# A conditioned mixture-of-experts layer on one core: a new order of ScalarE's work while the expert weights are split, and a rotated loop over the routed tiles

## The reference

```python
c  = einsum('btd,od->bto', x, W) + (einsum(x, A[idx]) @ Bm[idx]) * scalings[idx]   # c: 4096 x 512
sh = einsum('ted,edh->th', gelu(einsum('th,ehd->ted', c, Wsh_up)), Wsh_down)       # 2 shared experts
probs = softmax(c @ W_router); top_v, top_i = top_k(probs, 2)
gate = sum(one_hot(top_i, 16) * top_v[..., None], axis=1)
rt = einsum('ted,edh->th', gelu(einsum('th,ehd->ted', c, Wrt_up)) * gate[:, :, None], Wrt_down)
out = x + sh + rt
```

## Time and profile before

| | |
|---|---|
| time, median of 3 runs | 681.92 us (681.80 to 685.59) |
| the profiled execution's own time | 681.92 us |
| span of its trace | 679.9 us |
| PE busy | 627.5 us, 92% |
| DVE busy | 457.4 us, 67% |
| ACT busy | 327.2 us, 48% |
| POOL busy | 222.6 us, 33% |
| mean granted TensorE clock | 0.974 |

### The profile page before, as it was taken

One profiled execution on the slowest core, in us unless ns is written; L12 is line 12 of the kernel. 1 busy time (PEld: TensorE's weight loads), 2 busy tenths in 40 slices (PEclk: granted clock), 3 DMA queues, 4 the chain that ended last, 5 costly groups with the idle time before them and its releaser, 6 DMA issues.

```text
span 679.9 us, 13742 instructions
## 1 busy us (share of the span) xinstructions
PE 627.5 (92%) x4115; PEld 428.4 (63%) x4117; DVE 457.4 (67%) x900; ACT 327.2 (48%) x480; POOL 222.6 (33%) x288
## 2 busy tenths in 40 slices
PE   4998999999989758889999999999999999989794
PEld 2465656566657435556777777777777777665561
DVE  2779999999974998525555555555555554688674
ACT  1333224677775743464555555555555554333230
POOL 1000000101012742373333333333333306777771
PEclk9997999999998988999999999999999999999898
DMA  7688994343334312165555555555555539989966
GB/s 275 281 312 286 374 346 168 123 157 142 132 127 128 124 63 93 32 217 171 159 159 169 161 154 159 164 168 157 156 159 167 164 107 377 366 301 362 369 205 248
DMA packets 49765, 135.68 MB, mean 200 GB/s; under 512 B 6160, under 2 KB 6288, under 8 KB 47312
## 3 DMA queue, kind: packets, MB, share of 16 engines
q1 hardware_dynamic: 38304, 97.93, 39.1%
q0 software_dynamic: 11440, 37.50, 20.0%
HBM read 86.38 MB, written 49.02 MB: 199 GB/s over the span
## 4 chain that ended last, share of the span: by engine, by line
PE 53%; DVE 17%; POOL 12%; issue 7%; DMA 7%; ACT 1%; SPq 0%; DVEq 0%; POOLq 0%; ACTq 0%
PE bank L1412 15%; PE bank L1393 14%; POOL rtw L608 9%; PE bank L1249 7%; PE bank L1377 5%; DVE lot_max L906 5%; DMA act_in<-xT 3%; PE bank L1402 2%; PE bank L1327 2%; PE bank L1257 2%; PE bank L1274 2%; DMA region<-xc_dram,slot_idx 2%; PE bank L1238 1%; DVE x_max L947 1%; PE bank L1265 1%
## 5 line engine op out<-in xcount | busy, mean ns | idle before, releaser
L1129 DVE SCALAR_TENSOR_TENSOR region<-bank,scale,region 128x512 f16<-128x512 f32 x79 | 59.2, 751 | 128.7 <-ACT region L809 128.7
L1393 PE MATMUL bank<-rtw,region 128*128 x948 | 116.4, 273 | 0.0
L1412 PE MATMUL bank<-rtw,tmp 128*128 x474 | 115.2, 379 | 0.6 <-DVE tmp L1137 0.6
L1393 PEld LDWEIGHTS bank<-rtw,region 128*128 128x128 f16 x948 | 92.8, 98 | 10.1
L1340 PE MATMUL bank<-shw,hid 128*128 128x512 f16 x384 | 91.3, 397 | 8.3 <-DVE rtw L1193 7.7
L574 POOL DMA_INDIRECT region<-xc_dram,slot_idx x79 | 77.1, 976 | 61.3 <-POOL slot_idx L571 61.3
L1327 PE MATMUL bank<-act_in,shw 128*128 128x256 f16 x768 | 89.4, 277 | 2.9 <-ACT tmp L756 1.7
L1327 PEld LDWEIGHTS bank<-act_in,shw 128*128 128x128 f16 x768 | 75.8, 100 | 16.0 <-ACT tmp L756 2.2
L816 ACT ACTIVATE region<-bank,un_dn 128x512 f32<-128x512 f32 x79 | 54.3, 687 | 57.3 <-PE bank L1412 54.8
L608 POOL DMA_INDIRECT rtw<-r_dram,row_idx x64 | 70.0, 1093 | 27.6 <-issue 14.8
L1340 PEld LDWEIGHTS bank<-shw,hid 128*128 128x128 f16 x384 | 38.4, 102 | 56.4 <-issue 10.0
(11 more groups left out here) (157 smaller groups left out, 910.0 us busy)
## 6 DMA issues: line engine op xcount, KB each, us to landing
r_dram<-region SPq DMA_DIRECT2D x79, 256.0 KB
rtw<-rt_w SPq DMA_DIRECT2D x16, 1024.0 KB, 7.4
act_in<-xT SPq DMA_DIRECT2D x16, 512.0 KB, 3.8
xc_dram<-rows SPq DMA_DIRECT2D x16, 512.0 KB, 3.7
xcT_dram<-hid SPq DMA_DIRECT2D x16, 512.0 KB, 2.8
rtw<-x_rows SPq DMA_DIRECT2D x16, 512.0 KB, 5.4
rtw<-xcT_dram SPq DMA_DIRECT2D x13, 512.0 KB, 6.1
out<-rtw SPq DMA_DIRECT2D x9, 512.0 KB, 5.6
```

Of the source, the lines that this page charges most:

```text
L1129: nc.vector.scalar_tensor_tensor(xgT[s][:, 1], R_XT[s][:].rearrange("p (k t) -> p k t", k=HK), col(scale, C_ALL).bitcast(F32), xgT[s][:, 0 ...
L1393: last = mm(R_UP[s][:, 0:D], xgT[s][:, xp, k, :], rtw[:, bass.ds(e, 1), w0:w0 + D].rearrange("p a d -> p (a d)"), start=(k == 0 and n == 0 ...
L1412: last = mm(R_DN[s][:], midT[s][:, xp, m, :], rtw[:, bass.ds(e, 1), w0:w0 + H].rearrange("p a h -> p (a h)"), start=(m == 0 and n == 0), s ...
```

## The change

It has two parts. In ACT's program, for chunks 8 to 15, the first of the two `high_routed` of a step moves ahead of `high_x`, the second directly behind it, and `cond_T` comes after both, directly ahead of `cond_rows`. In step 8, `high_x(9)` stays first, then one `high_routed`, `cond_T(7)`, the other, `cond_rows(8)`. In step 15, `high_condT(0)` comes ahead of `cond_T(14)`. In PE's program the round over two routed tiles begins with `r_transpose_mid` instead of `r_down`, and three registers are loaded instead of four; the loop has 36 rounds instead of 35.

```diff
-            def routed_step(i, s, more=True):
-                c = 2 * i + s
-                if more:
-                    high_x(c + 1, 1 - s)
-                cond_T(c - 1, i - 1 + s, 1 - s)
-                for e in range(2):
-                    high_routed(2 * c - NC + e)
-                if not more:
-                    high_condT(0, 0, C_EARLY, early=True)
-                cond_rows(i, s)
-
             high_x(NC // 2 + 1, 1)
+            act.wait_ge(scale_ready, 3)
+            high_routed(0)
             cond_T(NC // 2 - 1, A_HALF // 2 - 1, 1)
-            act.wait_ge(scale_ready, 3)
-            for e in range(2):
-                high_routed(e)
+            high_routed(1)
             cond_rows(A_HALF // 2, 0)
+
+            def routed_step(i, s):
+                high_routed(4 * i - NC + 2 * s)
+                high_x(2 * i + s + 1, 1 - s)
+                high_routed(4 * i - NC + 2 * s + 1)
+                cond_step(i, s)
+
             routed_step(A_HALF // 2, 1)
...
             for s in range(2):
-                routed_step(A_HALF - 1, s, more=s == 0)
+                high_routed(E_RT - 4 + 2 * s)
+                if s == 0:
+                    high_x(NC - 1, 1)
+                high_routed(E_RT - 3 + 2 * s)
+                if s:
+                    high_condT(0, 0, C_EARLY, early=True)
+                cond_step(A_HALF - 1, s)
...
-                    tile_e[0:1, bass.ds(i, 1), 0:4]...
+                    tile_e[0:1, bass.ds(i, 1), 0:3]...
...
-            def r_round(i, first=False):
+            def r_pair(i, first=False, more=True):
                 e = r_experts(i)
                 for s in range(2):
                     j = 2 * i + s
-                    r_down(j, s, e[s], first)
-                    r_transpose_mid(j + 1, 1 - s, first and s == 0)
-                    r_up(j + 2, s, e[2 + s])
-                    r_transpose_x(j + 4, i + 2, s)
+                    r_transpose_mid(j, s, first and i == 0)
+                    r_up(j + 1, 1 - s, e[s + 1], first and i == 0 and s == 0)
+                    if more:
+                        r_transpose_x(j + 3, i + 1 + s, 1 - s)
+                    if first and i == 0 and s == 0:
+                        pe.wait_ge(shared_ready, NT * EARLY)
+                    r_down(j, s, e[s], first and i == 0)
...
-            e = r_experts(0)
-            r_up(0, 0, e[0], first=True)
+            r_up(0, 0, r_experts(0)[0], first=True)
             r_transpose_x(2, 1, 0)
-            r_transpose_mid(0, 0, first=True)
-            r_up(1, 1, e[1], first=True)
-            r_transpose_x(3, 1, 1)
-            pe.wait_ge(shared_ready, NT * EARLY)
             for i in range(2):
-                r_round(i, first=(i == 0))
-            with pe.Fori(2, NJ_2 - 2) as i:
-                r_round(i)
...
+                r_pair(i, first=True)
+            with pe.Fori(2, NJ_2 - 1) as i:
+                r_pair(i)
+            r_pair(NJ_2 - 1, more=False)
+
+            e = r_experts(NJ_2)
             r_transpose_mid(NJ - 1, 0)
             shared_up(EARLY // 2, 0, blocks=range(1))
-            r_down(NJ - 1, 0, e[2])
+            r_down(NJ - 1, 0, e[0])
```

More of the change, by code:

```diff
@@ L1382, in r_experts @@
                 return nc.values_load_multi_w_load_instructions(
-                    tile_e[0:1, bass.ds(i, 1), 0:4].rearrange("p a m -> p (a m)"), engines=(mybir.EngineType.PE,), min_val=0, max_val=E_RT - 1,
+                    tile_e[0:1, bass.ds(i, 1), 0:3].rearrange("p a m -> p (a m)"), engines=(mybir.EngineType.PE,), min_val=0, max_val=E_RT - 1,
                     skip_runtime_bounds_check_because="a count of experts, cut off at the last one by the vector engine")[1]
```

## The result

The changed kernel takes 745.75 us (median of 4 runs, 742.05 to 749.36), the one before 683.75 us in the same session: a ratio of 1.0906, 95% interval 1.0838 to 1.0976. The forecast was 726 with a range of 708 to 740. The direction and the mechanism of ScalarE's part came out, the size did not: some 20 us come from TensorE's part, which I had priced at nothing.

A forecast was written before the change was run, and what follows sets the result against it. In chunks 8 to 15 PE was taken as the bound, DVE nearly full; routed tiles were a gapless PE rhythm. 681.9 + 26.8 (loop) + 17.6 (clock) + 0 (tile order) = 726.3, forecast 726 us, range 708 to 740.

The forecast's parts named there:

- The closed loop: Chunks 8 to 15: PE, DVE and ACT wait in a ring, 14.9 us a step against 10.86; +26.8 us at full clock.
- The view of the waits: Steps 8 to 15: ACT waits for DVE directly ahead of `cond_T`, no longer for PE's transposes; DVE waits for `high_x`.
- the reversal of who waits for whom: Steps 8 to 15: PE's router waits for DVE, DVE for ACT, and ACT for PE through `cond_rows`; no separate size.
- the stage view: Steps 8 to 15 were to show 15 to 19 us each, PE idle 3 to 5 us ahead of the first router matmul.
- one sign: Steps 8 to 15: DVE was to be seen waiting for ACT's `high_x`; no size given.
- Part 1: ACT's new order in steps 8 to 15: +26.8 us from the loop and +17.6 us from the clock.
- Rival (c): Steps 8 to 15: the stall is paid only at the start, +7 us, 689 us; chance 0.07.
- (d): Steps 8 to 15: early `high_routed` fills ACT's idle time and PE's 1.29 and 2.08 us bubbles vanish, 678.5 us; chance 0.03.
- The clock: Steps 8 to 15: PE's clock falls after each of 8 stalls, 2.2 us each, +17.6 us; bounds 0 and 26.9.
- Rival (a): Steps 8 to 15: the loop closes but PE keeps its clock or pays a small ramp, 709 to 716 us; chance 0.14.
- Part 2: Routed tiles: PE's reordered loop end stays hidden, 0 us over 36 rounds; bounds a gain of 0 and a loss of 7.2.
- Rival (b): Routed tiles: the loop-end work is not hidden, 733 us, or 745 at full exposure; chance 0.12.

The follow-up runs named there:

- e7: e1 plus 14 extra unused matmuls on PE ahead of each router product in steps 8 to 15; 712.4 us, ratio 1.0472 to the kernel before.
- e5: e1 with `high_x` moved ahead of the first `high_routed` from step 9 on; 721.9 us, ratio 1.0592 to the kernel before.
- e10: e5 plus 10 extra matmuls in PE's idle time ahead of the router; 701.3 us, ratio 1.0304 to the kernel before.
- e1: The kernel before with only ScalarE's (ACT's) new order, TensorE's loop unchanged; 731.3 us, ratio 1.0674.
- e9: ScalarE's part alone, `cond_T` between the two `high_routed` from step 9 on, step 8 in its old order; 681.1 us, ratio 0.9967.

## Why the prediction was wrong, point by point

**The closed loop: right, in place and in size.** At full clock the step was to be 14.9 us; the steps of the changed kernel less their clock share are 14.92 and 14.95, e7 has one of 15.0. The view of the waits, the reversal of who waits for whom, and the stage view came as described, but for one sign: DVE waited for `high_x` in four steps only, 3.1 us in all. Part 1 alone is +46 us where the sum of its terms was 44.4; so close a total is luck in part, since the loop's term was too large and the clock's too small, as the next point shows. Rival (c), a stall only at the start, and (d), the other side, fall by the same rows: each of the 8 routers waits.

**The clock: right in kind, sized too small.** The term was 8 x 2.2 = 17.6 us. From router to adapter inputs the 8 pairs took 6.54, 6.76, 6.98, 6.44, 6.82, 6.99, 5.06 and 6.33 us, less 3.50 each: together 23.9 us, 3.0 a stall. I had thought that part of each low stretch would fall in slack; mostly it did not, and the value lay near the bound of 3.36. In return the rest of the stage came to 47.9 - 23.9 = 24.0 us, not 26.8; 1.1 of that is step 8, where the scales came earlier against PE's work (router +2.4 us, not +3.5), and 1.5 is step 9, which took 14.8 us less its clock share, not 16.3: the rows of chunk 8 waited for PE's slow adapter products, so some of the low stretch did fall in slack there. Rival (a) falls. The Trainium skill's rule ("TensorE: Matmul & The Clock Gate", section "What's actually happening"), which puts the ramp under 1% of a typical kernel's span, does not fit this kernel: 23.9 of 748.7 us are 3.2%.

**Part 2: wrong, and this carried the forecast out of its range.** The step that failed reads: "I take 0 over 36 rounds, because the nearest row is the unchanged 3.26", with 36 x 0.2 = 7.2 as the upper bound. It was 20.0 us, 36 x 0.55 = 19.8 of it at the loop's ends (a round of 7.07 us in the mean, not 6.52). Two things were wrong in it. I used the 333 ns of a load of four values for a load of three, and took fewer values to be cheaper or equal; the trace had no row for three, and I did not bound that cost. And the upper bound was made from a wait recorded in the old place, where the slack was other than in the new one, though I had noted that weight load and matmul of D begin together and so nothing is to spare. Rival (b) was the right kind (a part 2 that is not hidden), with 733 to 745 us, and its case was left half outside the range. Its price came from full exposure at 0.54 a round; the exposure is in fact partial, of a longer piece of work (branch and load take 1.16 us), so that 0.54 is so near to 0.55 is luck. Against the trace, whose own time is 750.7 us, the forecast of 726.3 is short by 24.4: 20.0 from part 2, 6.3 from the clock and 0.9 from elsewhere, less the 2.8 by which the loop was priced too high.

**A later miss of the same sort.** In e5 I summed one branch of a loop that has two of nearly the same length. It did not show in the prediction, because the branch that I followed was the longer one at full clock: the steps are 15.0 us with it (e7) and 13.95 without (e10), and in e7's step at full clock `x_low` waits 0.97 us for `high_x`.

## What to carry to other kernels

When an in-order engine serves two others, ask of every piece that is moved ahead of another whether it waits for work that in the same step depends on the piece it displaced; if so, all engines settle at the loop's own length, which can be summed from rows, and every branch must be summed. A stall that repeats can be paid twice, once as idle time and once as the low clock behind it: here 23.6 us of waits ahead of the router products and 23.9 us of slower router and adapter products. A sequencer's instructions are priced with their operands: a load of three values is not a cheaper load of four, and where weight load and matmul begin together behind a loop's end, there is little slack to put anything in.

## What the runs showed of the hardware that I had not expected

The time of a load of values into TensorE's registers does not follow the number of values: medians of 0.33 us for four, 0.54 for two and 0.78 for three in the same place (the last two as the first of a pair). Behind the down products it takes 0.17 us more (0.50 for four, 0.95 for three). As the second of two loads in a row, one value has a median of 0.70 us and two values 0.87, up to 1.3. Why the three widths stand in this order is open; no run here separates the number of values from the form in which they are fetched.

And extra matmuls in an idle TensorE shortened the kernel: 14 x 8 of them took e1 from 1.0674 to 1.0472 of the time before.

How long a wait brings the low clock is open: in e9 0.82 us ahead of the router products was followed by a granted clock of 0.52 over the adapter products, in e7 0.86 us by one of 0.66, while before the change 2.52 us ahead of 24 dense matmuls brought no fall. No run here varies the length of the wait by itself.
